# One bank-count load and wait for four groups of edges, in the layer-0 aggregation of a graph network kernel

## The reference

```python
attn = ex / jnp.maximum(denom[dst], 1e-10)
out = jax.ops.segment_sum(h_src * attn[..., None], dst, num_segments=n)
return out.reshape(n, H * D) + bias
```

## Time and profile before

| | |
|---|---|
| median of 3 runs | 3079.68 us (3078.61 to 3094.67) |
| span of the profiled execution | 3595.1 us |
| time of the profiled execution beside its span | not given apart from the span |
| PE busy, of the span | 2251.7 us (63%) |
| DVE busy, of the span | 2033.2 us (57%) |
| last matmul of the stage starts | 1252.3 us |

### The profile page before, as it was taken

How to read it: one execution, slowest core, us unless ns; L and a number is a source line. 1 busy time by engine, 2 the same in 40 slices (tenths; PEclk the granted TensorE clock), 3 DMA queues, 4 the chain that set the end, 5 groups by cost and what they waited for, 6 DMA issues and landing times. The chain is left out here.

```text
span 3595.1 us, 47970 instructions
## 1 busy us (share of the span) xinstructions
PE 2251.7 (63%) x11012; PEld 1557.3 (43%) x11013; DVE 2033.2 (57%) x4073; ACT 1091.0 (30%) x3339; POOL 1519.1 (42%) x1534
## 2 busy tenths in 40 slices
PE   3333567677578738976666498897703556666543
PEld 3112233333456535553455377675602434444432
DVE  6328455556788844325268577677504645555733
ACT  3103232333300122215200465664400055556311
POOL 1660544453000020112453777775472166666044
PEclk9755566655799959998867799998855677777577
DMA  4870555565287628862697787786686344444066
GB/s 140 227 203 0 157 176 178 166 184 170 93 237 230 195 86 258 268 221 92 242 392 255 231 249 245 242 245 203 186 220 172 85 126 128 127 130 130 7 203 192
DMA packets 450407, 655.70 MB, mean 182 GB/s; under 512 B 68320, under 2 KB 329310, under 8 KB 449683
## 3 DMA queue, kind: packets, MB, share of 16 engines
q1 hardware_dynamic: 330003, 351.74, 31.7%
q0 software_dynamic: 84944, 255.17, 24.1%
q10 hardware_dynamic: 35296, 46.90, 3.7%
HBM read 485.21 MB, written 169.74 MB: 182 GB/s over the span
## 5 line engine op out<-in xcount | busy, mean ns | idle before, releaser
L1603 POOL DMA_INDIRECT xn<-table,src_col x572 | 617.5, 1080 | 246.1 <-issue 155.7
L1646 PE MATMUL sum_h_ps<-xn,sum_h_hot 128*128 128x261 f32 (+1 forms) x1936 | 556.4, 439 | 226.3 <-DVE xn L1660 103.2
L1646 PEld LDWEIGHTS sum_h_ps<-xn,sum_h_hot 128*128 128x128 f32 x1936 | 404.2, 217 | 369.5 <-issue 169.9
L1160 POOL DMA_INDIRECT arena_a<-table,src_col x264 | 268.0, 1015 | 388.9 <-issue 321.1
L1669 DVE TENSOR_TENSOR arena_a<-arena_a,sum_h_ps 128x522 f32 (+1 forms) x440 | 246.4, 560 | 305.2 <-issue 115.4
L1033 POOL DMA_INDIRECT arena_b<-table,al x272 | 257.5, 947 | 360.1 <-ACT arena_a L1072 185.5
L1054 PE MATMUL score_ps_hd<-arena_a,score_hot 128*128 x1320 | 289.4, 382 | 0.0
L1110 DVE TENSOR_TENSOR xn<-xn,score_ps_hd 128x528 f32<-128x528 f32 x220 | 154.4, 702 | 228.1 <-remote 144.5
L1660 DVE TENSOR_TENSOR xn<-xn,al 128x514 f32<-128x514 f32 (+1 forms) x352 | 242.9, 690 | 45.8 <-issue 19.4
L1754 PE MATMUL sum_ps<-xn,sum_hot 128*128 128x264 f32 x880 | 210.6, 393 | 52.2 <-DVE sum_hot L1764 34.2
L1050 PE MATMUL score_ps_en<-enc_rows,score_attr 30*128 30x256 bf16 x440 | 119.4, 367 | 186.5 <-DVE xn L1110 122.5
(11 more groups left out here) (531 smaller groups left out, 4127.5 us busy)
## 6 DMA issues: line engine op xcount, KB each, us to landing
xn<-edge_h SPq DMA_DIRECT2D x220, 264.0 KB, 3.0
edge_h<-arena_b SPq DMA_DIRECT2D x68, 528.0 KB
arena_b<-kept SPq DMA_DIRECT2D x66, 516.0 KB
xn_t<-edge_rows SPq DMA_DIRECT2D x110, 256.0 KB, 4.7
score_h_hot<-hots SPq DMA_DIRECT2D x220, 128.0 KB
kept<-arena_a ACTq DMA_DIRECT2D x40, 516.0 KB
xn<-kept SPq DMA_DIRECT2D x66, 257.0 KB
arena_a<-in_f_w SPq DMA_DIRECT2D x16, 1024.0 KB, 8.6
```

What stands on the lines that cost most here:

```text
L1160: pool.indirect_dma_start(rows[:, q, s, :], None, table, bass.IndirectOffsetOnAxis(ap=K.src_col[:, w * SUB + s:w * SUB + s + 1], axis=0)). ...
L1603: pool.indirect_dma_start(rows[w][:, s, 0:RW], None, table, bass.IndirectOffsetOnAxis(ap=K.src_col[:, w * SUB + s:w * SUB + s + 1], axis=0 ...
L1646: ins = pe.matmul(ps[:, u, b, 0:part], lhsT=hot[:, w % QH, s, :], rhs=rows[w][:, s, b * part:(b + 1) * part], start=(s == 0), stop=(s == S ...
```

## The change

PE no longer loads the four numbers of row 0. It loads one, that of the last of the four windows (the largest of them, as the tiles come in order), and waits for it once, ahead of the four windows. The waits on `s_hot` and `s_msg` stay. The other engines are not touched.

```diff
                     if j % 4 == 0:
-                        needs = load_four(pe, K.bank[0:1, 0, bass.ds(w, 4)], 1, NT)
                         banks = load_four(pe, K.bank[0:1, 1, bass.ds(w, 4)], 0, BANKS - 1)
+                        need = pe.value_load(K.bank[0:1, 0, bass.ds(w + 3, 1)], min_val=1, max_val=NT)
+                        pe.wait_ge(s_free, need)
                     pe.wait_ge(s_hot, w + 1)
                     pe.wait_ge(s_msg, w + 1)
-                    pe.wait_ge(s_free, needs[j % 4])
```

## The result

| | before | after |
|---|---|---|
| median of 6 runs | 3081.99 us (3078.61 to 3094.95) | 3055.31 us (3051.05 to 3065.97) |
| ratio to before | 1 | 0.9899, 95% interval 0.9881 to 0.9917 |
| span of the profiled execution | 3595.1 us | 3049.3 us |
| matmuls of the stage, first to last start | 259.3 us | 227.0 us |

The change makes the kernel 1.0% faster, 31 us by the ratio and 27 us by the medians. The forecast was 3052 us, 28 us less than before, with a range of 3042 to 3078.

What follows compares the result with a forecast made beforehand. PE's queue, 4.61 us per four windows, was taken as the bound, falling to 3.35 to 3.85; then DVE and SP at 1.049 us a window save 28.9 us; less 1, 3079.7 − 28 = 3052 us, range 3042 to 3078.

Steps and rivals of the forecast that it cites:

- PE's queue is the bound, not DVE or DMA: In the changed stage, PE's instruction queue sets the pace: 4.61 us per four windows, 1.153 us a window.
- The sum: Stage's end: last message at 992.02 + 219 × 1.049 = 1221.7 us, last pass ending 1223.8, not 1252.7; 28.9 us saved.
- the transfers' least time for a window: Load queue of the stage: DMA engines 77.9% busy at 1.153 us a window, so at least 0.90 us a window.
- The register load is the cost, and the waits next to nothing: PE's queue per four windows: load of four counts removed, 1.65 us; waits save 0 to 0.4, new wait costs 0 to 0.1.
- A load of one costs nearly what a load of four costs: PE's register load: 0.30 us for one number against 0.33 for four; with its checks, one costs 0.79 us.
- DVE is late next, with SP close behind: After the change, per four windows: DVE 4.04 us (1.011 each) binds, SP's queue needs 4.0 us.
- 1.049 us a window in the coupled stage: Pace of DVE and SP after the change, modelled on the stage's start: 17 windows in 17.83 us.
- The saving stands on the path: Barrier at the stage's end: DVE waits 7.49 us for PE's drain, so the whole 28.9 us counts.
- Recording as a rival: PE's queue in the stage is slow only while recorded; gain 0 to 10 us, 3075 us; chance 0.24.
- Transfers as a rival: DMA loads become the stage's bound, 1.10 us a window; 18 us saved, 3062 us; chance 0.12.
- The dear single load: PE's load of one value costs 1.26 us, period 4.8 us; 10 us slower, 3090 us; chance 0.04.
- A wait on the freed banks: The bound moves from PE's queue to a wait on freed banks at tile borders; no change; chance 0.03.

Runs made afterwards that it cites:

- the DVE edit: Both one-hot matrices built in one DVE operation: on the changed kernel 3045.56 us, ratio 0.9882; with SP's range checks also removed 3034.21 us, ratio 0.9853.

## Why the prediction was right, point by point

- *PE's queue is the bound, not DVE or DMA.* Shown. Taking register work out of that queue in two different ways (one count in place of four; no checks on the bank numbers) gave 227.0 and 226.9 us of stage, and nothing else was touched. The pace was misread by the loop's turn: 52 periods of 4.70 us on the mean, not 53 of 4.61. The sum did not use the count, since it started from the last pass as read; the transfers' least time for a window did, and by the mean of 1.187 us from issue to issue over those 260 us it is 0.92 us and not 0.90.
- *The register load is the cost, and the waits next to nothing.* Shown by the two halves: 259.2 us with only the waits moved, 227.5 with only the load cut. The sum put 0 to 0.4 us a period on the waits; The lower end was wrong in kind: a window with two waits keeps both instructions that carried its three. PE's queue had room for that error, since its new need of 3.35 to 3.85 us lay below the 4.05 of the others.
- *A load of one costs nearly what a load of four costs.* 0.306 against 0.332 us. That is the TENSOR_LOAD alone; with its register rows a checked load of one takes about 0.8 us of the queue (825.4 to 826.2 us in the changed kernel), as in the sum, and one of four 1.65. The page's floor of 600 ns for a `tensor_load` (the Trainium skill, "DMA: Bandwidth & Descriptors", section "Latency and other measured facts") is not seen here, by half. What the page says beside it is that the compiler unrolls four times to spread that cost; the load of four in the prediction is my reading of it.
- *DVE is late next, with SP close behind.* This step named the wrong bound, though the numbers were near. SP at 1.020 us a window sets the stage, and DVE's 1.011 is 1% behind. Of SP I summed four issues and a load, 4.0 us, and left out its turn of the loop; that is how 1.00 became 1.020. SP's issues took 223.5 us in the changed kernel and again with a faster DVE, so neither PE nor DVE held it up.
- *1.049 us a window in the coupled stage.* This term was mis-sized. The model, the stage's first 17 windows, has more waits than the stage as a whole: DVE's messages measured 1.029 us, which puts the last of them 4.4 us earlier than the sum had it. Against that, the last pass ended 3.0 us after the last message began, not 2.1. Hence 32.3 us less in the stage where 28.9 were worked out. That the forecast of 28 us came so near is in part luck: 1.049 was taken from DVE's start and not from what then held the stage.
- *The saving stands on the path.* The barrier follows PE's drain. DVE's wait for it fell from 7.49 to 3.3 us, and the time fell by 31 us (ratio) or 27 (medians) for the stage's 32.
- *Recording as a rival, 0.24.* It was wrong: the second profile of before, with recording on, has a span of 3078.6 us. A profile whose span is far from the median may be one odd execution.
- *Transfers as a rival, 0.12.* Wrong too. The stage went on to 0.956 us a window, 282 GB/s for 270 KB; so the estimate of 240 GB/s between two sizes of the page's table (the same page of the Trainium skill, section "Bandwidth") doesn't hold here. The page's table was measured on loads issued from GpSimd. These are issued from SP, with several in flight, and no run tells which of the two matters.
- *The dear single load, 0.04.* Its longest was 0.319 us; it did not occur. The stage has 55 such loads, not 219 as the prediction says.
- *A wait on the freed banks, 0.03.* It did not bind: in the whole stage PE waited 0.4 us for ACT's clearing of banks, in two places.

## What to carry to other kernels

A gap of one size that comes once in every n pieces of work, where the code reads registers, points at the engine's own queue, even where the profile names another engine as releaser: add up that queue's small operations, and the loop's turn with them, before looking further. Count the register operations behind a load, not only the load: in this kernel a checked number cost about 0.29 us on PE, and dropping the checks of a table that the kernel itself builds in range gave as much as the change. When several queues lie within 1 or 2% of each other, an edit to one can show next to nothing until the others are moved too: the DVE edit gave 0.4 us on the changed kernel and 12 us once SP was relieved.

## What was not expected of the hardware

In this stage of the changed kernel a TENSOR_LOAD of four numbers from SBUF took 0.29 to 0.35 us, but for one of SP's that took 0.53, and one of a single number took 0.302 to 0.319. One of ten numbers took 0.94 to 2.09 us (22 of them on SP, median 1.63). Where between four and ten it turns, and why, was not tried; nor was ten on PE.
